# Chunk recurrence: corrections in two sets, a turned PE loop, new orders on DVE, ACT and GpSimd, a smaller filler

## The chip, the cores and the metric

The kernel runs on one core of a Trainium2 chip. A core has five engines with an instruction queue each: PE (TensorE, matmuls and the loading of their weights), DVE (VectorE), ACT (ScalarE), POOL (GpSimd) and SP (SyncE, which here issues transfers). They run on their own and wait for one another on semaphores. The metric is device time in microseconds (us), the median over runs.

## What is computed

Four images of 256 channels and 32 x 32 positions pass two residual layers; both see a group normalisation of their input. The first is the one that the change touches. Its tokens (4 x 1024) are projected to queries, keys and values of 8 heads with 32 columns, and a recurrence over 64 chunks of 16 tokens carries a small matrix `W1` (32 x 32) and a row `b1` for every head and image:

```python
def step(carry, inp):
    W1c, b1c = carry
    xq, xk, xv, et = inp
    Z1 = xk @ W1c + b1c
    grad = _ln_l2_bwd(Z1, xv - xk, g, bb)
    Attn1 = jnp.tril(xq @ xk.swapaxes(-1, -2))
    b1_bar = b1c - jnp.tril(et) @ grad
    Z1_bar = xq @ W1c - et * Attn1 @ grad + b1_bar
    last_eta = et[..., -1, :, None]
    W1n = W1c - (last_eta * xk).swapaxes(-1, -2) @ grad
    b1n = b1c - (last_eta * grad).sum(-2, keepdims=True)
    return ((W1n, b1n), xq + _ln(Z1_bar, g, bb, EPS_IN))
...
x = x + _L0_conv_ref(_gn(x), ...)   # the recurrence, then a layer norm and a projection
x = x + _L1_conv_ref(_gn(x), ...)   # a 5 x 5 self-correlation, a 1 x 1 convolution, relu
```

`grad` is the gradient of a layer norm's squared error: it needs the row sums of `Z1` and of its square, and two more sums of products.

## The kernel before

All 32 pairs of image and head are worked on together: a tile of a chunk has 128 partitions (4 groups of 2 heads x 16 tokens) and 4 x 32 = 128 columns (images x head columns). Ahead of the recurrence stand the group norm, the layer norm and the projections; behind it a layer norm, the output projection and the second layer. In the recurrence every engine runs one list of instructions, chunk after chunk, in an order written out by hand; semaphores in the dictionary `q` carry a count for each step. Only PE has a loop there: chunks 0 and 1, then a loop whose body holds four chunks (it runs 15 times, with a branch back after each), then chunks 62 and 63. The other engines' lists are written out for all 64 chunks.

In chunk c the steps run as follows (names as in the code, lines as in the profile).

- PE, function `body`: waits for the gradient `GL` of chunk c-1 (count `gl`), its mask products (`am`) and ACT's copy of the key products (`s1`). It then adds the correction by that gradient to `Z` of chunk c, which already stands in a PSUM bank (`grads`, L1167, 32 matmul passes); updates `W1` and `b1` (`update`, L1179 and L1187); adds the attention part to the queries' bank of chunk c-1 (`grads` again, L1167); issues `filler`, a matmul of the identity by 256 columns whose result nobody reads (L1194, two passes); computes `base`, that is `Z` of chunk c+1 by the state so far with the products of its keys (L1152) and the bias (L1158); and `qbase`, the queries of chunk c by the state (L1231). The branch back of the loop stands after `qbase`, ahead of the corrections.
- ACT: the square of `Z` (L1556); `out_store`, which copies a finished transposed chunk `ZT` into `TT` (L1548); a square for the output norm (L1538); a root (L1562) and a variance (L1565); copies of the new `W1` and `b1` from PSUM for PE (L1497, L1501); in chunks 40 to 47 a `gain` over 512 columns (L803); then keys and queries for later matmuls (L1508 two instructions, L1524 two, L1517) and `products`, the copy of the key products of chunk c+1 that is counted in `s1` (L1531); last a root for the output norm (L1544).
- DVE: sums of the square and of `Z` (L1300, L1301), `PZ`, `ZC`, `TS` (L1302 to L1308), a reciprocal (L1314), `y` (L1319), `yp`, `my`, `m` (L1322 to L1325), two 4-wide products `cc0` and `cc1` (L1328, L1332), `YC` (L1336), `WX` (L1338), and the gradient `GL` = `WX` + `YC` (L1341). Behind it, for older chunks: a sum for the output norm (`out_var`, L1284), `out_turn` (the transposition of `ZN` into `ZT`, L1294) and `out_rows` (L1279).
- POOL: `u`, `u2` (L1423, L1426) and `YL` (L1428); in chunk 56 a `pre` over 512 columns (L1449); `blocks`, the keys of chunk c+2 spread for PE's `base` (L1395); `masks`, the mask products of chunk c+1 (L1411); `out_norm`, which writes `ZN` of chunk c-3 (L1419) once the turn of chunk c-4 has read it; `queries`, a copy for chunk c+2 (L1403).
- SP issues transfers that wait for counts of `gl` and `khx`.

## Time and profile before

| what | us |
|---|---|
| median of 3 runs (583.01 to 584.29) | 583.49 |
| the profiled run | 581.06 |
| its span, first to last instruction | 579.2 |
| chunk 0's square to the last gradient | 282.71 |

The profile is one execution on the chip. Each row of its timeline has a start and a duration in us from the span's start, the engine, the line of the program, the operation, what it writes and reads, the count of instructions merged into the row and, in brackets, how long the engine had been idle and what ended that. PE is the matmuls and PEld the loading of weights; matmuls overlap one another, and their ends are modelled. "issue" as a releaser means that the profile shows nothing that was waited for. The granted clock is a share of 2.4 GHz.

### The profile page before, as it was taken

How to read it: one execution, taken by the hardware profiler on the slowest of the kernel's cores; microseconds unless marked ns; L12 is line 12 of the kernel's file. 1: busy time of each engine (PE TensorE's matmuls, PEld its weight loads, DVE VectorE, ACT ScalarE, POOL GpSimd, SP SyncE). 2: the span in 40 equal slices, each digit the busy share in tenths (PEclk: the TensorE clock that was granted, in tenths of full speed). 3: DMA queues.
4: the chain of work that ended last, by engine and by line, in shares of the span. 5: the costliest groups of instructions: out<-in, count | busy, mean ns of one | idle time of the engine just before them, and what ended most of it. 6: DMA issues, size and time to landing. Idle time of an engine off the chain costs nothing.

```text
span 579.2 us, 30352 instructions
## 1 busy us (share of the span) xinstructions
PE 483.9 (84%) x12556; PEld 313.8 (54%) x12556; DVE 432.1 (75%) x1526; ACT 346.2 (60%) x1166; POOL 327.8 (57%) x590
## 2 busy tenths in 40 slices
PE   0699889898558789888888888888887699998996
PEld 0344334443346577777777676666675244456563
DVE  4757788888746789888888888888885667676652
ACT  2344334322246788888888889988885487553321
POOL 1276888787734466666666655565763667330112
PEclk9999989899858999999999999999997899998998
DMA  8310111111101011111111000011010500000123
GB/s 338 123 24 14 37 37 36 38 36 36 39 9 32 22 37 28 33 32 33 33 28 37 1 1 1 19 36 37 19 37 4 171 1 2 1 2 1 74 75 145
DMA packets 15136, 24.74 MB, mean 43 GB/s; under 512 B 4228, under 2 KB 4968, under 8 KB 15080
## 3 DMA queue, kind: packets, MB, share of 16 engines
q1 hardware_dynamic: 15080, 24.10, 13.8%
q8 instruction: 23, 0.38, 0.3%
q14 instruction: 33, 0.27, 0.2%
HBM read 11.50 MB, written 4.19 MB: 27 GB/s over the span
## 4 chain that ended last, share of the span: by engine, by line
PE 25%; DVE 24%; ACT 12%; issue 8%; POOL 2%; POOLq 0%; ACTq 0%
PE PS L1167 6%; PE PS L924 4%; PE PS L1255 3%; PE PS L906 3%; ACT work L1556 3%; PE PS L361 2%; DVE work L1341 2%; DVE work L1336 2%; DVE work L1322 2%; DVE work L1300 2%; DVE work L1319 2%; DVE PS L1338 2%; DVE PS L1323 2%; DVE PS L1302 2%; DVE PS L1325 2%
## 5 line engine op out<-in xcount | busy, mean ns | idle before, releaser
L1167 PE MATMUL PS<-work 32*32 32x32 f32 x4064 | 59.6, 194 | 37.9 <-DVE work L1341 21.0
L1167 PEld LDWEIGHTS PS<-work 32*32 32x32 f32 x4064 | 53.8, 108 | 43.4 <-issue 43.1
L1411 POOL TENSOR_TENSOR work<-work,mask 128x256 f32<-128x256 f32 x64 | 46.8, 731 | 35.7 <-ACT work L1531 35.7
L512 PE MATMUL PS<-X,work 128*128 128x512 f32 x128 | 63.2, 641 | 0.3 <-ACT X L435 0.3
L1423 POOL TENSOR_TENSOR work<-work,lrh 128x4 f32<-128x4 f32 x64 | 12.9, 201 | 75.6 <-DVE work L1314 70.1
L1300 DVE TENSOR_REDUCE work<-work 128x4 f32<-128x128 f32 x64 | 18.3, 286 | 49.2 <-ACT work L1556 49.2
L663 POOL TENSOR_TENSOR work<-work 128x512 f32<-128x512 f32 x32 | 43.8, 1370 | 7.1 <-DVE work L582 7.1
L1152 PEld LDWEIGHTS PS<-work 64*32 64x32 f32 x2048 | 32.9, 110 | 24.9 <-issue 23.6
L1152 PE MATMUL PS<-work 64*32 64x64 f32 x2048 | 43.6, 225 | 2.9 <-issue 2.0
L1194 PE MATMUL PS<-cst 128*128 128x256 f32 x126 | 45.1, 440 | 0.0
L1179 PE MATMUL PS<-work 32*64 32x32 f32 x2016 | 43.0, 222 | 2.2 <-issue 2.2
L1508 ACT ACTIVATE work<-TK,small 128x128 f32<-128x128 f32 x128 | 44.3, 402 | 0.0
L1524 ACT ACTIVATE work<-QP,cst 128x128 f32<-128x128 f32 x128 | 43.9, 396 | 0.0
L1395 POOL TENSOR_TENSOR work<-KP,cst 128x256 f32<-128x256 f32 x64 | 39.2, 612 | 6.5 <-POOLq L454 6.5
L512 PEld LDWEIGHTS PS<-X,work 128*128 128x128 f32 x128 | 25.3, 206 | 29.5 <-issue 28.7
L881 POOL TENSOR_TENSOR TK<-TK 128x512 f32<-128x512 f32 x7 | 9.0, 1304 | 53.5 <-ACT TK L1077 53.5
L1179 PEld LDWEIGHTS PS<-work 32*64 32x64 f32 x2016 | 35.8, 135 | 3.9 <-issue 1.3
L581 DVE TENSOR_TENSOR work<-PS,work 128x512 f32<-128x512 f32 x32 | 21.8, 683 | 21.4 <-POOL KP L666 19.1
L1544 ACT ACTIVATE work<-work,small 128x4 f32<-128x4 f32 x64 | 19.0, 296 | 24.7 <-DVE work L1284 24.6
L377 ACT ACTIVATE work<-X 128x512 f32<-128x512 f32 (+1 forms) x16 | 9.7, 630 | 40.0 <-DVE X L368 40.0
L1255 PE MATMUL PS<-TK,wsm 128*128 128x512 f32 x64 | 31.4, 616 | 1.5 <-ACT X L1600 1.5
L1158 PE MATMUL PS<-work,cst 128*128 128x128 f32 x128 | 32.2, 334 | 0.0
(162 smaller groups left out, 1344.5 us busy)
## 6 DMA issues: line engine op xcount, KB each, us to landing
X<-in_x SPq DMA_DIRECT2D x4, 1024.0 KB, 8.2
TK<-KP SPq DMA_DIRECT2D x64, 64.0 KB, 1.9
X<-QP SPq DMA_DIRECT2D x64, 64.0 KB, 2.0
TK<-in_x SPq DMA_DIRECT2D x16, 256.0 KB, 3.0
out<-TK SPq DMA_DIRECT2D x16, 256.0 KB, 2.4
work<-in_rope SPq DMA_DIRECT2D x2, 512.0 KB, 9.1
cst<-in_consts SPq DMA_DIRECT2D x1, 289.0 KB, 5.0
work<-in_wk SPq DMA_DIRECT2D x1, 256.0 KB, 11.2
```

Source lines behind the costliest of these rows:

```text
L512: mm = nc.tensor.matmul(PS[:, 2 + m, :], lhs(j), xt(i, j), start=(j == 0), stop=(j == J - 1))
L663: nc.gpsimd.tensor_tensor(ksw[:, t, :], ksw[:, t, :], sinT[:, h], ALU.mult).then_inc(s_ksin, 1)
L1152: mm = nc.tensor.matmul(PS[HD * a:HD * a + HD, ZB[p], b * ZW:b * ZW + ZW], KT2[p][r:r + 64, k * B + b, :, :].rearrange("p e t -> p (e t)") ...
L1158: nc.tensor.matmul(PS[:, ZB[p], 0:B * ZW].rearrange("p (b n) -> p b n", b=B)[:, :, 0:HD], ident, Bs[1 - p if past(n, 1) else 0], start=Fal ...
L1167: mm = nc.tensor.matmul(PS[HD * a:HD * a + HD, bank, b * width:b * width + HD], AM[p][HD * a:HD * a + HD, b, part, :, :].rearrange("p e t ...
L1179: mm = nc.tensor.matmul(PS[2 * HD * a2:2 * HD * a2 + 2 * HD, WB + k, b * HD:b * HD + HD], KHX[p][HD * a:HD * a + HD, b, :, :].rearrange("p ...
L1194: nc.tensor.matmul(PS[:, QB[p], 256:512], ident, ccol("spread", 0, 256), start=True, stop=True, skip_group_check=True)
L1255: mm = nc.tensor.matmul(PS[:, 2 + m, :], wsm[:, j, m * P:(m + 1) * P], ot(i, j), start=(j == 0), stop=(j == J - 1))
L1395: nc.gpsimd.tensor_tensor(KT2[p], chunk(KP, c).unsqueeze(2).broadcast_to([P, J * B, E, CS]), ccol("emask_k").unsqueeze(1).unsqueeze(3).bro ...
L1411: nc.gpsimd.tensor_tensor(AM[p].rearrange("p b s e t -> p (b s) e t"), S1[p].unsqueeze(2).broadcast_to([P, 2 * B, E, CS]), mask2.rearrange ...
L1508: kx = nc.scalar.activation(KHX[p][:, :, e, :].rearrange("p b (f t) -> p b f t", f=E), head_rows(1, c), ACT.Copy, scale=upd_mask[:, e:e + 1])
L1524: a = nc.scalar.activation(QT2[p][:, :, e, :], chunk(QP, c), ACT.Copy, scale=ccol("emask_k", e, 1))
```

## The change

- The corrections are two sets of 32 passes: `YC` first, once `yc`, `am` and `s1` are there, then `WX` once `w` is there. `GL` is still computed, for `update` and the attention part, which now wait for `gl`. `WX` moves from PSUM to SBUF.
- PE's body is cut into `front` (corrections, update, attention, filler) and `back` (`base`, `qbase`), and the loop runs back, front: four backs and four fronts a pass, with the branch back after a front. Prologue and epilogue are written out around it.
- `filler` has 128 columns instead of 256, and the fourth front of each pass has none; nor has the one after the loop.
- DVE: `my` ahead of `yp`, `cc0` and `YC` ahead of `cc1`, `out_var` between `WX` and `GL`.
- `out_turn` writes `TT` itself; ACT's `out_store`, the tile `ZT` and the counts `zt` are gone, and `out_norm` waits for `ot`.
- POOL: after `YL` come `out_norm` and `queries`, then a wait for `gl` of this chunk, `masks`, `blocks`.
- ACT: the two `qt2` copies (L1524) stand behind `products`.

The diff, cut to its core:

```diff
@@ -776,8 +776,8 @@
             return PS[:, 7, at * B * HD:(at + 1) * B * HD].rearrange("p (b d) -> p b d", b=B)
 
 
-        PZ, WX, ZC = (home(at) for at in range(3))
-        at = 3 * B * HD
+        PZ, ZC = (home(at) for at in range(2))
+        at = 2 * B * HD
         cc0, sums = PS[:, 7, at:at + B], PS[:, 7, at + B:at + 3 * B]
 
...
@@ -1191,39 +1181,15 @@
 
                 def filler(p):
 
-                    nc.tensor.matmul(PS[:, QB[p], 256:512], ident, ccol("spread", 0, 256), start=True, stop=True,
+                    nc.tensor.matmul(PS[:, QB[p], 256:384], ident, ident, start=True, stop=True,
                                      skip_group_check=True)
 
...
-                run_chunks(pe, body)
+                def front(p, before, done, now, fill):
+
+                    o = 1 - p
+                    pe.wait_ge(q["init"], 1)
+                    pe.wait_ge(q["yc"], done)
+                    pe.wait_ge(q["am"], done)
+                    pe.wait_ge(q["s1"], now)
+                    grads(ZW, ZB[p], o, 1, YC)
+                    pe.wait_ge(q["init"], 1)
+                    pe.wait_ge(q["w"], done)
+                    grads(ZW, ZB[p], o, 1, WX).then_inc(q["corr"], 1)
+                    pe.wait_ge(q["init"], 1)
+                    pe.wait_ge(q["gl"], done)
+                    pe.wait_ge(q["khx"], done)
+                    pe.wait_ge(q["bcopy"], done)
+                    update(o)
+                    grads(HD, QB[o], o, 0, GL[o]).then_inc(q["attn"], 1)
+                    if fill:
+                        if before is not None:
+                            pe.wait_ge(q["zq"], before)
+                        filler(p)
+
+                def back(c, p, before, now, nxt):
+
+                    if not is_last(c):
+                        base(c + 1, 1 - p, nxt, now)
+                    else:
+                        pe_mean(pe, 0, True)
+                    query_base(now, p, before)
+
+                base(0, 0, 1, 1)
+                back(0, 0, None, 1, 2)
+                front(1, None, 1, 2, True)
+                back(1, 1, None, 2, 3)
+                front(0, 1, 2, 3, True)
+
+                with nc.Fori(0, NC // 4 - 1, engines=(mybir.EngineType.PE,), hint_back_edge=True) as four:
+                    for k in range(4):
+                        c, p = four * 4 + (2 + k), k % 2
+                        before, done, now, nxt = (value(pe, c + n) for n in (-1, 0, 1, 2))
+                        back(c, p, before, now, nxt)
+                        front(1 - p, done, now, nxt, k < 3)
+                back(NC - 2, 0, NC - 3, NC - 1, NC)
+                front(1, NC - 2, NC - 1, NC, False)
+                back(NC - 1, 1, NC - 2, NC, None)
...
@@ -1291,8 +1301,9 @@
                 def out_turn(c):
 
                     dve.wait_ge(q["zn"], c + 1)
-                    nc.vector.transpose(ZT.rearrange("p b d -> p (b d)"), ZN.rearrange("p b d -> p (b d)")
-                                        ).then_inc(q["zt"], 1)
+                    nc.vector.transpose(
+                        TT.rearrange("p e (b n) -> p b e n", b=B)[:, :, :, c * CS:(c + 1) * CS],
+                        ZN.rearrange("p b (e t) -> p b e t", e=E)).then_inc(q["ot"], 1)
 
                 def body(c, p):
                     zb = PS[:, ZB[p], 0:B * ZW].rearrange("p (b n) -> p b n", b=B)[:, :, 0:HD]
...
                     dve.wait_ge(q["y"], c + 1)
                     dve.wait_ge(q["zc"], c + 1)
+                    nc.vector.tensor_reduce(sums[:, 0:B], YY[:, 0, :, :], AX.X, ALU.add).then_inc(q["my"], 1)
                     nc.vector.tensor_tensor(YY[:, 1, :, :], YY[:, 0, :, :], ZC, ALU.mult).then_inc(q["yp"], 1)
-                    nc.vector.tensor_reduce(sums[:, 0:B], YY[:, 0, :, :], AX.X, ALU.add).then_inc(q["my"], 1)
-                    dve.wait_ge(q["yp"], c + 1)
-                    nc.vector.tensor_reduce(sums[:, B:2 * B], YY[:, 1, :, :], AX.X, ALU.add).then_inc(q["m"], 1)
                     dve.wait_ge(q["u"], c + 1)
                     dve.wait_ge(q["my"], c + 1)
                     nc.vector.scalar_tensor_tensor(cc0, sums[:, 0:B], -1.0 / HD, lead[:, 0, :],
                                                    ALU.mult, ALU.mult).then_inc(q["cy"], 1)
+                    dve.wait_ge(q["yp"], c + 1)
+                    nc.vector.tensor_reduce(sums[:, B:2 * B], YY[:, 1, :, :], AX.X, ALU.add).then_inc(q["m"], 1)
+                    dve.wait_ge(q["yl"], c + 1)
+                    dve.wait_ge(q["cy"], c + 1)
+                    nc.vector.tensor_tensor(YC, YL, bc(cc0), ALU.add).then_inc(q["yc"], 1)
                     dve.wait_ge(q["m"], c + 1)
                     dve.wait_ge(q["u2"], c + 1)
                     nc.vector.scalar_tensor_tensor(cc1, sums[:, B:2 * B], -1.0 / HD, lead[:, 1, :],
                                                    ALU.mult, ALU.mult).then_inc(q["c"], 1)
-                    dve.wait_ge(q["yl"], c + 1)
-                    dve.wait_ge(q["cy"], c + 1)
-                    nc.vector.tensor_tensor(YC, YL, bc(cc0), ALU.add).then_inc(q["yc"], 1)
                     dve.wait_ge(q["c"], c + 1)
                     nc.vector.tensor_tensor(WX, ZC, bc(cc1), ALU.mult).then_inc(q["w"], 1)
-                    dve.wait_ge(q["w"], c + 1)
                     dve.wait_ge(q["yc"], c + 1)
-                    nc.vector.tensor_tensor(GL[p], WX, YC, ALU.add).then_inc(q["gl"], 1)
-
                     if past(c, 2):
                         out_var(c - 2)
+                    dve.wait_ge(q["w"], c + 1)
+                    nc.vector.tensor_tensor(GL[p], WX, YC, ALU.add).then_inc(q["gl"], 1)
+
                     if past(c, 4):
                         out_turn(c - 4)
                     if past(c, 1):
...
@@ -1415,7 +1422,7 @@
 
                 def out_norm(c, p):
                     if past(c, 1):
-                        pool.wait_ge(q["zt"], c + 0)
+                        pool.wait_ge(q["ot"], c + 0)
                     nc.gpsimd.tensor_tensor(ZN, ZQ[c % 3], bc(sdq[1 - p]), ALU.mult).then_inc(q["zn"], 1)
...
@@ -1428,14 +1435,16 @@
                     nc.gpsimd.tensor_tensor(YL, YY[:, 0, :, :], bc(lead[:, 0, :]), ALU.mult).then_inc(q["yl"], 1)
                     if c == PRE_AT:
                         pre(0)
-                    if not near_end(c):
-                        blocks(c + 2, p)
-                    if not is_last(c):
-                        masks(c + 1, 1 - p)
                     if past(c, 3):
                         out_norm(c - 3, 1 - p)
                     if not near_end(c):
                         queries(c + 2, p)
+
+                    pool.wait_ge(q["gl"], c + 1)
+                    if not is_last(c):
+                        masks(c + 1, 1 - p)
+                    if not near_end(c):
+                        blocks(c + 2, p)
 
                 for c in range(2):
...
-
                 def body(c, p):
                     zb = PS[:, ZB[p], 0:B * ZW].rearrange("p (b n) -> p b n", b=B)[:, :, 0:HD]
                     if past(c, 1):
                         act.wait_ge(q["corr"], c + 0)
                     nc.scalar.activation(SQ, zb, ACT.Square).then_inc(q["sq"], 1)
-                    if past(c, 5):
-                        out_store(c - 5)
                     if past(c, 2):
...
@@ -1573,12 +1574,11 @@
                         act.wait_ge(q["ot"], NC // PER)
                         gain(act, i, j).then_inc(q2["in"], 1)
                     khx(c, p)
-                    if not is_last(c):
-                        qt2(c + 1, 1 - p)
                     if not isinstance(c, int) or c + 3 < NC:
                         next_k(c + 2, p)
                     if not is_last(c):
                         products(c + 1, 1 - p)
+                        qt2(c + 1, 1 - p)
                     if past(c, 2):
                         out_sd(c - 2, p)
 
```

## Rows read from the trace of the kernel before

**Rows 1.** Busy time by stretch: us, five engines' busy time (instructions), clock, DMA share, GB/s.
```profile
167.69:199.27 31.58, 23.13 (x942) 18.02 (x938) 20.64 (x101) 20.67 (x81) 15.09 (x40) 0.86 0.12 29
199.27:433.48 234.21, 203.83 (x9469) 162.56 (x9470) 201.42 (x990) 198.35 (x834) 147.37 (x387) 1.00 0.10 25
433.48:450.40 16.92, 13.31 (x422) 9.82 (x419) 10.36 (x52) 9.05 (x38) 5.82 (x17) 0.80 0.02 6
```

**Rows 2.** Timeline of one steady chunk (start, us, engine, line, operation, operands, count).
```profile
253.48 0.28 ACT L1556 ACTIVATE work<-PS 128x128 f32<-128x128 f32 x1
...
254.18 0.47 PE L1167 MATMUL PS<-work 32*32 32x32 f32 x32
...
254.50 0.42 ACT L1497 ACTIVATE work<-PS 128x128 f32<-128x128 f32 x2
...
254.58 0.70 PE L1194 MATMUL PS<-cst 128*128 128x256 f32 x2
254.58 0.29 DVE L1308 TENSOR_TENSOR work<-TK,work 128x128 f32<-128x128 f32 x1
254.78 0.20 DVE L1314 RECIPROCAL work<-work 128x8 f32<-128x8 f32 x1
...
255.06 0.20 POOL L1423 TENSOR_TENSOR work<-work,lrh 128x4 f32<-128x4 f32 x1 [1.03 <-DVE work L1314]
...
255.21 0.65 PE L1152 MATMUL PS<-work 64*32 64x64 f32 x32
...
255.85 0.61 POOL L1395 TENSOR_TENSOR work<-KP,cst 128x256 f32<-128x256 f32 x1
...
256.30 0.29 DVE L1338 TENSOR_TENSOR PS<-PS,work 128x128 f32<-128x128 f32 x1
256.34 0.36 ACT L1531 ACTIVATE work<-PS,small 128x128 f32<-128x128 f32 x1
256.63 0.29 DVE L1341 TENSOR_TENSOR work<-PS,work 128x128 f32<-128x128 f32 x1
256.77 0.73 POOL L1411 TENSOR_TENSOR work<-work,mask 128x256 f32<-128x256 f32 x1 [0.31 <-ACT work L1531]
...
257.02 0.45 PE L1167 MATMUL PS<-work 32*32 32x32 f32 x32 [0.36 <-DVE work L1341]
257.03 0.30 DVE L1294 STREAM_TRANSPOSE work<-work 128x128 f32<-128x128 f32 x1
...
257.40 0.67 PE L1179 MATMUL PS<-work 32*64 32x32 f32 x32
257.46 0.40 POOL L1419 TENSOR_TENSOR work<-work 128x128 f32<-128x128 f32 x1
257.54 0.28 ACT L1556 ACTIVATE work<-PS 128x128 f32<-128x128 f32 x1
...
257.80 0.29 POOL L1403 COPY work<-QP 128x128 f32<-128x128 f32 x1
```

**Rows 3.** Timeline in a chunk with `gain`: products, and the corrections that they release.
```profile
349.22 0.36 ACT L1531 ACTIVATE work<-PS,small 128x128 f32<-128x128 f32 x1
...
349.72 0.45 PE L1167 MATMUL PS<-work 32*32 32x32 f32 x32 [0.88 <-ACT work L1531]
```

**Rows 4.** Timeline: the first corrections behind the loop's branch back.
```profile
265.62 0.45 PE L1167 MATMUL PS<-work 32*32 32x32 f32 x32 [0.83 <-POOL work L1411]
```

**Rows 5.** Busy time by stretch: chunks 2 to 5, the loop's first pass.
```profile
178.68:199.27 20.59, 15.59 (x697) 12.13 (x698) 14.21 (x70) 13.91 (x58) 10.22 (x28) 1.00 0.12 29
```

**Rows 6.** Timeline: corrections of chunk 62, just behind the loop.
```profile
437.13 0.32 PE L1167 MATMUL PS<-work 32*32 32x32 f32 x15 [0.47 <-DVE work L1341]
440.55 0.44 PE L1167 MATMUL PS<-work 32*32 32x32 f32 x17 [3.11 <-issue]
```

**Rows 7.** Timeline in chunk 57, where POOL is late by its `pre`.
```profile
416.33 0.62 POOL L1395 TENSOR_TENSOR work<-KP,cst 128x256 f32<-128x256 f32 x1
...
416.67 0.42 DVE L1308 TENSOR_TENSOR work<-TK,work 128x128 f32<-128x128 f32 x1
```

69 lines of the change are left out of this document (12 added, 57 removed).

## Prediction

> **What bounds the kernel now.** I read first the busy time by stretches [rows 1]. The span of 579.2 us falls into a front part (167.69 us), the recurrence over 64 chunks (282.71 us, cut here at the squares of chunk 0, 6 and 61 and at the last gradient) and a back part (128.80 us). Only the recurrence is edited. In its middle stretch 55 chunks take 234.21 us, 4.26 each, with no engine busy all the time: a loop of waits, not an engine, sets the pace.
>
> Second, the timeline of one steady chunk [rows 2]. Let S be the start of the ACT square L1556, 253.48; the next is at 257.54, so a chunk is 4.06. The loop that ends last runs square, sums and elementwise work on DVE, WX (L1338, S+2.82), GL (L1341, S+3.15 to 3.44), the correction matmuls L1167 (S+3.54), next square. But three others are close behind, and the whole question is which comes next:
> - ACT and PE: state copy L1497 ends at S+1.44, base L1152 at S+1.73 (just when the filler L1194 lets it go), products L1531 1.13 after it, S+2.86 to 3.22. They let the corrections go 0.14 later [rows 3], at S+3.36, so 0.18 of slack against S+3.54.
> - GpSimd: the key blocks L1395 at S+2.37, masks L1411 at S+3.29, query normalisation L1419 0.69 later. The blocks are done more than two us before the base that reads them. That is much slack.
> - PE itself: in every fourth chunk the loop jump stands between the query base and the corrections; L1167 is then idle 0.83 [rows 4] in place of 0.36 [rows 2], so that chunk costs 0.47 more: four chunks 4 x 4.06 + 0.47 = 16.71.
>
> Third, the two ends. The first pass over PE code is slow: 1395 matmuls and weight loads in 20.59 us [rows 5], 14.8 ns each, four chunks at 5.15. Where PE leaves the loop, it stops 3.11 us inside a correction, waiting for nothing that is recorded [rows 6], and the clock of that stretch is 0.80 on the mean [rows 1].
>
> **The change part by part.**
>
> *Two-set corrections.* GL (WX + YC) leaves the path: PE takes YC first, then WX. On DVE the same instructions stand between the sums and WX; `my` now needs a finished `y` and the two 4-wide products stand apart, so WX starts some 0.06 later, at S+2.88, ends S+3.17 and could reach PE at S+3.27 (GL to L1167 took 0.10 [rows 2]). Alone this would shorten the chunk by 0.27. But PE has 32 matmuls more, 0.38 (L1167 to L1179 [rows 2]), and the first set waits for the products too.
>
> *The ACT and PE loop then.* The 128-column filler takes half of 0.63, so it ends at S+1.41 and no longer holds the base; the state copy does: 1.44 + 0.14 = S+1.58. The products follow 1.13 after it, as before, with the bias between them: S+2.71. ACT is free by then, as the two query copies now stand behind the products. Products 0.36, to PE 0.14: the YC set starts at S+3.21, the WX set at S+3.59, and its square follows 0.52 later (257.02 to 257.54): 4.11. WX had been ready 0.3 earlier. So what GL gives, the second set takes: 4.11 against 4.06.
>
> *GpSimd's new order.* Normalisation and query copy now come before masks and blocks, and the masks get a wait for GL. Queued behind that wait are masks and blocks; the base of the next chunk waits for the blocks. Yet the added wait is not the late one: `out_norm(c-3)` waits for `out_turn(c-4)`, which DVE runs after GL(c). Before, blocks and masks filled that time; now they queue behind it. WX S+2.88, two DVE slots (0.40 for two, L1341 to L1294) to GL at 3.28, turn 3.48 to 3.78, to GpSimd 0.08 (L1314's end to L1423): normalisation S+3.86, copy +0.35, masks +0.29, blocks +0.69 at S+5.19, done S+5.80, PE 0.14 later: S+5.94. If the next chunk starts at S+4.11, that is its +1.83, and its base was wanted at +1.58. From base to the following square is 4.11 - 1.58 = 2.53, so two chunks cost 8.47, not 8.22.
>
> *TS under the blocks.* The blocks now run at +1.08 to +1.69 of the next chunk, just when DVE's TS (L1308) starts at +1.10. The one place of the trace where blocks and TS overlap shows TS at 0.42 us [rows 7], against 0.29 in the steady chunk [rows 2]: +0.13, which everything up to the turn inherits: 8.60 for two chunks. The Trainium skill, "SBUF — State Buffer", section "SBUF: two separate sides", calls the port pair of VectorE and GpSimd an exclusive lock, also for a VectorE operation with two SBUF inputs, as TS is; by that rule TS would end only after the blocks, up to 0.45 later, and the fours below would cost about 0.3 more. The one overlap agrees in kind.
>
> *Turned loop.* The jump now stands between the attention matmuls and the base. Attention L1167 ends at S+1.17 (254.18 + 0.47); plus 0.83 is S+2.00 against 1.58: +0.42 in that chunk, which has no filler. It stays on the path: the pair with it is 2 x 4.11 + 0.42 = 8.64. Four chunks: 8.64 + 8.60 = 17.24, or 17.11 without the TS stretch, against 16.71. For some 47 ordinary chunks (64 less 6 at the head, 8 with `gain`, 3 at the tail), 11.75 fours: +4.7 to +6.2. I take +5.5, nearer to the end with the stretch, since a row shows it.
>
> *Chunks with gain* (8): there the products are last (idle 0.88 before L1167 [rows 3], so 4.58). From the state copy to the products ACT works 1.84 without a break on eight instructions [rows 2]; two of them move behind, an estimate of 0.5. With the second set (+0.38) that leaves -0.15 a chunk: -1.2 in all (0 to -2).
>
> *First pass.* 64 PE instructions more a chunk at 14.8 ns: 0.95 for each of four chunks in the loop, and 0.8 for chunk 1 and the loop's new entry: +4.6. Bounds: +1, if this code is not what PE waits for, to +6.
>
> *Tail.* The exit now comes after front 62, so one front less is left for new code. The 3.11 stall may stand before the base of chunk 62 instead (gain 0) or vanish with the low clock behind it: 16.92 against three chunks of 4.2 and 0.3, so -4. I take -3, as PE ran on for 15 matmuls past the exit before it stopped. The Trainium skill, "Runtime: NRT & Kernel Launch", "Instruction fetch mechanics", has instructions come in blocks of 256; by that the rest of chunk 62 would be at hand already, which speaks for the lower end.
>
> *At nothing.* The ACT store (0.30) goes; ACT waits for the first sum after it anyway. The turn writes TT in 16-element runs: no row shows that on DVE; ACT wrote the same runs in 0.30 and TS reads them in 0.29, so 0, with 0.1 as upper bound (+2.4 in all). WX in SBUF: 0, other operands of this shape differ by 0.01. SP's transfers wait for GL counts that come within 0.2 of before; nothing waits for them here.
>
> *Sum.* +4.6 + 5.5 - 1.2 - 3.0 = +5.9. The profiled run took 581.06 (span 579.2), 2.4 below the median 583.49 of the runs; so 587.0 for that run and 589.4 for the median.
>
> **The rivals.**
> 1. *The jump hides and GpSimd is in time (faster).* If PE's sequencer turns the loop while the attention matmuls run, and the blocks end before S'+1.44, only the 4.11 loop is left: fours of 16.44, -3.2 in 47 chunks, gains -1.5, tail -4, head +4: about -5, 578.5. It decides at whether the blocks end before the state copy. Against: the addition above misses that by 0.25, and the jump showed 0.83 of idle.
> 2. *It does what it says.* If the products are no limit and WX is last: -0.27 for some 58 chunks, -0.44 for 13 jumps, +4.6 at the head, -3 at the tail: -19.8, 563.7. Against: [rows 3] show the products letting PE go.
> 3. *The larger loop no longer stays at hand.* Four chunks hold 4 x 64 instructions more than now. If each pass must fetch its code again, each costs 1632 x 14.8 ns = 24.2 against 17.2, 14 times: +98; if only its first piece, 3.11 x 14 = +44: 630 to 690. For: first pass and exit show what fetching costs. Against: after its first pass, the present loop shows clock 1.00 and no such stop over 55 chunks. The skill's section on fetching gives PE room for 2048 instructions; about 1670 fit, if not by much in whole blocks.
> 4. *The clock falls to 1.2 GHz,* with a quarter and more of the filler gone. About 2.0 us of the 4.11 are PE's and would at most double; a tenth of the 64 chunks would be +12: 601. Against: the clock is 1.00 over the middle stretch, with jumps (idle 0.83) and gain chunks (0.88) in it, and 32 matmuls are added.
>
> **How the numbers follow.** Forecast 0.70, with 584 to 594 as its own range (head +1, no TS stretch; tail 0, turn 0.1 dearer); rival 1 0.12; rival 2 0.04; rival 3 0.08; rival 4 0.06. Some 0.2 % (1.2 us) is what a measurement can tell from no change. Faster: rivals 1 and 2 and a little of the forecast, 0.18; same: the forecast's lower end, 0.10; slower 0.72. The range 577.0 to 598 leaves out rivals 2 and 3, a quarter of rival 1 and most of rival 4.
>
> **What would show it.** Right: squares some 4.1 and 4.3 to 4.6 apart by turns, base released by GpSimd's blocks or the jump, the YC set by the products, GpSimd's normalisation by the turn, TS longer than 0.29. Wrong: squares 3.8 apart with the WX set released by L1338's successor; jump chunks no longer than others; stops of 3 us within the middle stretch; a clock below 1.00 there.

## The result, and the profile after

The changed kernel takes 597.85 us (median of four runs, 596.37 to 600.41) against 583.89 of before in the same comparison: ratio 1.0238, 95 % interval 1.0191 to 1.0285. The forecast was 589.4, slower by 5.9; it is slower by 14.0. The direction and the steady chunk were right, the size was not. The profiled execution of the changed kernel took 600.41 with a span of 598.6, against 581.06 and 579.2. Runs of one kernel of this family differ by up to some 3 % with the mean granted clock (one below took 583.21 at 0.941 and 601.41 at 0.906), so differences are read from stretches whose clock stands beside them.

First the busy time by stretch, cut at the ACT squares (L1559 now) of chunks 0, 6, 12, 57 and 60 and at the last gradient; then the stretch that the trace shows at the lower clock behind the first pass, the middle, and the one behind chunk 57. Columns as in [rows 1].

```profile
166.93:205.78 38.85, 29.00 (x1130) 24.31 (x1126) 20.38 (x101) 20.59 (x80) 15.05 (x40) 0.68 0.10 24
205.78:236.46 30.68, 28.59 (x1228) 24.45 (x1229) 21.59 (x108) 20.62 (x85) 14.37 (x39) 0.72 0.09 22
236.46:431.68 195.22, 170.84 (x9162) 145.52 (x9162) 172.58 (x811) 158.18 (x638) 121.34 (x317) 1.00 0.09 24
431.68:449.73 18.05, 16.05 (x615) 13.62 (x618) 11.01 (x55) 10.35 (x43) 10.19 (x26) 0.62 0.09 28
449.73:467.58 17.85, 15.02 (x685) 11.77 (x686) 14.27 (x71) 11.97 (x50) 8.51 (x23) 0.94 0.02 6
...
199.19:223.08 23.89, 23.05 (x754) 19.56 (x754) 14.30 (x72) 13.30 (x54) 9.46 (x26) 0.50 0.08 20
223.08:434.71 211.63, 184.78 (x9931) 157.58 (x9927) 185.66 (x875) 171.23 (x693) 131.74 (x342) 1.00 0.09 24
434.71:448.36 13.65, 12.92 (x443) 10.86 (x433) 8.77 (x45) 6.99 (x28) 6.35 (x18) 0.50 0.05 19
```

Beside the same cuts of before (its squares stand at 167.69, 199.27, 224.14, 415.57 and 429.41, its last gradient at 450.40):

| stretch | before | after | difference | forecast |
|---|---|---|---|---|
| ahead of chunk 0 | 167.69 | 166.93 | -0.8 | 0 |
| chunks 0 to 5 | 31.58 | 38.85 | +7.3 | +4.6 |
| chunks 6 to 11 | 24.87 | 30.68 | +5.8 | +0.7 |
| chunks 12 to 56 | 191.43 | 195.22 | +3.8 | +3.1 |
| chunks 57 to 59 | 13.84 | 18.05 | +4.2 | +0.4 |
| chunk 60 to the last gradient | 20.99 | 17.85 | -3.1 | -2.9 |
| behind | 128.8 | 131.0 | +2.2 | 0 |

(The forecast column spreads the +5.5 of 47 ordinary chunks evenly, and adds the -1.2 of the gain chunks to chunks 12 to 56.) Chunks 12 to 56 and the last ones up to the gradient agree within 0.7. The two that miss by most are those with a mean clock of 0.72 and 0.62: at 1.2 GHz TensorE is busy 23.05 of 23.89 us and sets the pace by itself, 6.1 us a chunk. The first six chunks (mean clock 0.68) miss by 2.7 and the part behind the recurrence by 2.2.

The timeline of two steady chunks, from square to square to square (the form of [rows 2]; the chunk of 4.16, then one of 4.48), with the base of the chunk ahead of them, which stands behind the jump:

```profile
264.43 0.65 PE L1142 MATMUL PS<-work 64*32 64x64 f32 x32 [0.90 <-POOL work L1402]
...
266.83 0.28 ACT L1559 ACTIVATE work<-PS 128x128 f32<-128x128 f32 x1 [0.17 <-PE PS L1157]
...
267.81 0.61 POOL L1402 TENSOR_TENSOR work<-KP,cst 128x256 f32<-128x256 f32 x1
...
267.93 0.64 DVE L1319 TENSOR_TENSOR work<-TK,work 128x128 f32<-128x128 f32 x1
...
268.52 0.65 PE L1142 MATMUL PS<-work 64*32 64x64 f32 x32
...
269.63 0.37 ACT L1540 ACTIVATE work<-PS,small 128x128 f32<-128x128 f32 x1 [0.42 <-PE PS L1148]
...
270.14 0.78 PE L1157 MATMUL PS<-work 32*32 32x32 f32 x64 [0.16 <-ACT work L1540]
...
270.63 0.30 DVE L1304 STREAM_TRANSPOSE TK<-work 128x128 f32<-128x128 f32 x1
...
270.99 0.28 ACT L1559 ACTIVATE work<-PS 128x128 f32<-128x128 f32 x1
271.02 0.40 POOL L1426 TENSOR_TENSOR work<-work 128x128 f32<-128x128 f32 x1 [1.42 <-DVE TK L1304]
...
272.09 0.40 DVE L1319 TENSOR_TENSOR work<-TK,work 128x128 f32<-128x128 f32 x1
...
272.30 0.67 POOL L1402 TENSOR_TENSOR work<-KP,cst 128x256 f32<-128x256 f32 x1
...
273.06 0.65 PE L1142 MATMUL PS<-work 64*32 64x64 f32 x32 [0.48 <-POOL work L1402]
...
274.17 0.37 ACT L1540 ACTIVATE work<-PS,small 128x128 f32<-128x128 f32 x1 [0.79 <-PE PS L1148]
...
274.68 0.74 PE L1157 MATMUL PS<-work 32*32 32x32 f32 x64 [0.16 <-ACT work L1540]
...
275.47 0.28 ACT L1559 ACTIVATE work<-PS 128x128 f32<-128x128 f32 x1 [0.16 <-PE PS L1157]
```

Read it against the forecast. The products L1540 let all 64 corrections go 0.14 after their end (TensorE was idle 0.16 by then); WX and GL are no longer last. GpSimd's normalisation L1426 waits 1.42 for DVE's turn L1304, so the key blocks L1402 come at +0.98 and +1.31 of the chunk, the base waits for them (S+2.07 in the second), and DVE's TS L1319 beside them takes 0.64 and 0.40 in place of 0.29 [rows 2]. The pair is 4.16 + 4.48 = 8.64; four chunks, one pass of the loop and called a four below, take 17.28. The forecast had 17.24, by the same steps.

### The profile page after: what moved, and what is told of

It reads as the page before. It is cut to its first block, busy times and chain, and to the rows that moved or that the text cites. A ratio compares the mean times of both kernels' runs of the same rounds, so it can differ in the third digit from the quotient of the medians.

```text
span 598.6 us, 34394 instructions
## 1 busy us (share of the span) xinstructions
PE 503.0 (84%) x14540; PEld 342.3 (57%) x14540; DVE 438.8 (73%) x1526; ACT 338.5 (57%) x1102; POOL 328.9 (55%) x590
## 3 DMA queue, kind: packets, MB, share of 16 engines
HBM read 11.50 MB, written 4.19 MB: 26 GB/s over the span
## 4 chain that ended last, share of the span: by engine, by line
PE 33%; issue 13%; POOL 13%; DVE 7%; ACT 6%; POOLq 0%; ACTq 0%
PE PS L1157 6%; PE PS L1142 4%; PE PS L924 4%; PE PS L1265 3%; PE PS L361 3%; PE PS L1148 3%; POOL work L1418 3%; POOL work L1402 3%; PE PS L906 3%; ACT work L1540 2%; POOL work L1426 2%; PE PS L1169 2%; POOL work L1435 2%; PE PS L946 1%; ACT work L1559 1%
## 5 line engine op out<-in xcount | busy, mean ns | idle before, releaser
L1157 PE MATMUL PS<-work 32*32 32x32 f32 x6080 | 82.5, 198 | 16.4 <-ACT work L1540 9.4
L1157 PEld LDWEIGHTS PS<-work 32*32 32x32 f32 x6080 | 76.7, 111 | 22.3 <-issue 21.2
L1426 POOL TENSOR_TENSOR work<-work 128x128 f32<-128x128 f32 x64 | 25.6, 400 | 90.4 <-DVE TK L1304 89.0
L1142 PE MATMUL PS<-work 64*32 64x64 f32 x2048 | 46.2, 233 | 22.4 <-POOL work L1402 18.0
L1142 PEld LDWEIGHTS PS<-work 64*32 64x32 f32 x2048 | 36.7, 116 | 31.9 <-issue 30.0
L1540 ACT ACTIVATE work<-PS,small 128x128 f32<-128x128 f32 x64 | 23.5, 367 | 48.2 <-PE PS L1148 47.8
L1169 PE MATMUL PS<-work 32*64 32x32 f32 x2016 | 45.3, 228 | 2.6 <-issue 2.4
L1402 POOL TENSOR_TENSOR work<-KP,cst 128x256 f32<-128x256 f32 x64 | 40.8, 637 | 5.8 <-POOLq L454 5.8
L1169 PEld LDWEIGHTS PS<-work 32*64 32x64 f32 x2016 | 39.0, 142 | 6.1 <-issue 2.5
L1148 PE MATMUL PS<-work,cst 128*128 128x128 f32 x128 | 34.6, 356 | 0.0
L1197 PE MATMUL PS<-work 64*32 64x32 f32 x2048 | 31.0, 202 | 0.7 <-issue 0.7
```

The lines of the kernel that those rows point to most:

```text
L1142: mm = nc.tensor.matmul(PS[HD * a:HD * a + HD, ZB[p], b * ZW:b * ZW + ZW], KT2[p][r:r + 64, k * B + b, :, :].rearrange("p e t -> p (e t)") ...
L1148: nc.tensor.matmul(PS[:, ZB[p], 0:B * ZW].rearrange("p (b n) -> p b n", b=B)[:, :, 0:HD], ident, Bs[1 - p if past(n, 1) else 0], start=Fal ...
L1157: mm = nc.tensor.matmul(PS[HD * a:HD * a + HD, bank, b * width:b * width + HD], AM[p][HD * a:HD * a + HD, b, part, :, :].rearrange("p e t ...
L1169: mm = nc.tensor.matmul(PS[2 * HD * a2:2 * HD * a2 + 2 * HD, WB + k, b * HD:b * HD + HD], KHX[p][HD * a:HD * a + HD, b, :, :].rearrange("p ...
L1402: nc.gpsimd.tensor_tensor(KT2[p], chunk(KP, c).unsqueeze(2).broadcast_to([P, J * B, E, CS]), ccol("emask_k").unsqueeze(1).unsqueeze(3).bro ...
L1426: nc.gpsimd.tensor_tensor(ZN, ZQ[c % 3], bc(sdq[1 - p]), ALU.mult).then_inc(q["zn"], 1)
```

## The experiments

**The filler's size.** The first question was whether the clock at half belongs to the smaller filler.

```
-PS[:, QB[p], 256:384], ident, ident, ...
+PS[:, QB[p], 256:512], ident, ccol("spread", 0, 256), ...
```

> The changed kernel with one size put back: the filler has 256 columns again, still in the same three of four chunks. Theory A (the smaller filler lets TensorE's clock fall in the first pass over the loop and behind the GpSimd stop of chunk 57): the granted clock is back at 1.00 by about chunk 5, the squares of chunk 0 and chunk 12 are 60 us apart in place of 69.5, the three chunks behind chunk 57's square take 14 in place of 18, and the steady fours stay at 17.3 (a filler twice as long ends at S+1.8, which only the chunks without late key blocks notice, +0.1): about 587 to 589 in all. Theory B (the stops of the longer first pass over new code hold the clock down, whatever the filler): the clock stays at 0.50 over chunks 5 to 8, 598 to 601.

Measured: 595.73 (594.93 to 596.24), ratio 1.0181. Chunks 6 to 11 took 26.1 (first row below) and chunks 57 to 59 13.89, at clock 1.00 both, as theory A has it; but chunks 0 to 5 still took 37.6, and in the middle stretch the clock fell twice, at chunks 22 and 42. So A holds for the stretch behind the first pass, and not for the first pass itself, and its total of 587 to 589 was missed. No filler at all:

```
-front(1 - p, done, now, nxt, k < 3)
+front(1 - p, done, now, nxt, False)
...
-front(1, None, 1, 2, True)
+front(1, None, 1, 2, False)
...
-front(0, 1, 2, 3, True)
+front(0, 1, 2, 3, False)
```

> The changed kernel without any filler matmul (the filler only writes a part of a bank that nothing reads). Theory A3 (the filler is what brings TensorE's clock back after a stop; with 256 columns chunks 6 to 11 took 26.1, with 128 columns 30.7): it stays at 0.50 for longer behind the first pass and behind chunk 57 than with 128 columns, and the middle stretch is no longer at 1.00 throughout either; chunks 6 to 11 take 33 or more, the total is over 605. Rival (the filler has nothing to do with it; the falls come by chance behind each stop): 592 to 600, chunks 6 to 11 at 30 to 31; the steady chunks gain nothing, as the base waits for the key blocks or the jump.

Measured: 602.09 (601.60 and 602.58). The clock fell in the middle stretch too, in chunks 36 and 52, mean 0.89 over 206.76 us. Chunks 6 to 11 took 28.7, not 33, and the total stayed below 605: these numbers of the theory missed. And the filler in all four chunks:

```
-front(1 - p, done, now, nxt, k < 3)
+front(1 - p, done, now, nxt, True)
...
-front(1, NC - 2, NC - 1, NC, False)
+front(1, NC - 2, NC - 1, NC, True)
...
-PS[:, QB[p], 256:384], ident, ident, ...
+PS[:, QB[p], 256:512], ident, ccol("spread", 0, 256), ...
```

> The changed kernel with the 256-column filler in all four chunks and in the last fronts too. Against the kernel with 256 columns in three of four (595.7, chunk with the jump 4.37 to 4.57). Theory of the forecast (the jump begins only when TensorE has done what stands before it, so the filler's 0.70 adds to it): the base behind the jump starts at about S+2.8 in place of S+2.1, one chunk in four grows by some 0.5, 599 to 602 if the clock holds as well. Rival (the sequencer turns the loop while the long matmul runs): base still at S+2.1, 592 to 596.

Measured: 593.66 (590.97 to 595.77). The rival won: the jump runs beside the long matmul. Busy time of chunks 6 to 11 with 256 columns, then of the middle stretch without filler, with 256 columns in three of four and in all four:

```profile
204.83:230.91 26.08, 23.13 (x1225) 19.12 (x1228) 22.25 (x108) 20.19 (x84) 14.36 (x40) 1.00 0.10 26
...
231.50:438.26 206.76, 172.38 (x9095) 149.09 (x9096) 170.60 (x811) 158.49 (x639) 122.42 (x320) 0.89 0.08 23
...
230.91:429.56 198.65, 180.15 (x9163) 147.79 (x9167) 169.43 (x810) 156.76 (x639) 121.48 (x317) 0.97 0.09 24
...
230.06:426.09 196.03, 183.38 (x9184) 148.09 (x9185) 170.42 (x810) 156.75 (x638) 121.33 (x317) 1.00 0.09 24
```

TensorE's timeline without filler, in chunk 36 (where the clock falls: the same 32 matmuls take 0.94, then 1.07; no jump stands there, the base waits for GpSimd's key blocks), then at the jump, in chunk 18, with 256 columns in three of four, and in all four:

```profile
337.18 0.94 PE L1142 MATMUL PS<-work 64*32 64x64 f32 x32 [0.89 <-POOL work L1402]
...
342.57 1.07 PE L1142 MATMUL PS<-work 64*32 64x64 f32 x32
...
258.93 0.65 PE L1142 MATMUL PS<-work 64*32 64x64 f32 x32 [0.93 <-POOL work L1402]
...
257.29 0.70 PE L1184 MATMUL PS<-cst 128*128 128x256 f32 x2
258.33 0.65 PE L1142 MATMUL PS<-work 64*32 64x64 f32 x32 [0.34 <-POOL work L1402]
```

From attention matmuls to base it is 1.39 without the filler (257.54 to 258.93) and 1.43 with it (256.90 to 258.33): 0.70 of matmul cost 0.04. (The key blocks end 0.22 to 0.26 ahead of these two bases. In the single-set kernels below they are done 3 us earlier, and the same distance is 1.40 without the filler, 1.43 and 1.37 with it.) TensorE then stands idle 0.34 at the jump, not 0.93, and in this kernel the clock stayed at 1.00 from chunk 6 to chunk 61. Even so it takes 11.0 more than the kernel before (593.66 against 582.65): its profiled execution has +4.2 over before's in chunks 0 to 5, +1.8 in chunks 6 to 11, +4.6 in chunks 12 to 56, -2.1 from chunk 60 on and +3.4 behind the recurrence.

The same small filler in the kernel before:

```
-PS[:, QB[p], 256:512], ident, ccol("spread", 0, 256), ...
+PS[:, QB[p], 256:384], ident, ident, ...
...
-body(four * 4 + (2 + k), k % 2)
+body(four * 4 + (2 + k), k % 2, k > 0)
```

> The kernel before with the filler of the change alone: 128 columns, in the same three of four chunks. Theory A (filler): the clock falls to 0.50 in the first pass or behind chunk 57 here too, and the time rises by 4 to 13, to 588 to 597; the steady chunks stay at 4.06, since there the gradients are last and not the base. Theory B (code stops of the longer first pass): the clock stays as in the kernel before, 584 within 1.

Measured: 615.03 (600.02 to 619.34), ratio 1.0538, more than either expectation. The middle stretch of the profiled execution (600.02) reads:

```profile
224.45:434.80 210.35, 185.90 (x7727) 156.14 (x7728) 164.44 (x810) 165.66 (x684) 121.06 (x317) 0.81 0.08 23
```

A mean of 0.81 over 210.35 us is 80 us at 1.2 GHz, nearly all in chunks 42 to 56, where chunks of 4.06 to 4.59 became 4.65 to 6.38. Its first pass is that of before (31.41 against 31.58). So the small filler lets the clock fall, and does nothing to the first pass.

**The changed kernel once more,** without an edit, to see what of the clock is fixed by the program.

> The changed kernel itself, a second profiled execution. If the falls of the clock are fixed by the program, it falls again at the same places (chunks 3, 5 to 8, 57 to 59), 597 to 600. If they depend on how a stop happens to fall in time, the steady chunks are again 4.16 and 4.47 by turns, but the length at 0.50 behind the first pass and behind chunk 57 differs from the first execution, and so does the time, by up to 6.

Measured: 593.60 and 603.75. The steady chunks are again 4.16 and 4.47 by turns; chunks 6 to 11 again took 31, at a mean clock of 0.71; but behind chunk 57 nothing fell this time (12.5 us for three chunks), and two falls in chunks 18 and 54 took its place (mean clock 0.93 over chunks 12 to 56, where the first execution had 1.00). So where it falls is left to the execution.

**GpSimd's order.** Back to the order of before, first without and then with the wait for GL ahead of the masks.

```
+blocks(c + 2, p)
+masks(c + 1, 1 - p)
 out_norm(c - 3, 1 - p)
 queries(c + 2, p)
-pool.wait_ge(q["gl"], c + 1)
-masks(c + 1, 1 - p)
-blocks(c + 2, p)
```

> The changed kernel with GpSimd's order of before alone: key blocks, masks, output normalisation, query copy, without the wait for GL. Theory of the forecast (the order sets the steady pace by the late blocks and by the lengthened TS): TS L1319 back at 0.29, base at S+1.6 in three of four chunks and at S+2.1 behind the jump, fours of 16.5 in place of 17.26, some 12 fours, so 588 to 590 if the clock of the first pass stays as it is. Rival (the two sets or the turned loop set the pace by themselves): fours of 17.1 to 17.3, 596 to 598.

Measured: 588.34 (584.06 to 598.46), ratio 1.0069: the time as expected, the fours not quite, 16.93 (3.99, 4.19, 3.99, 4.76) for 16.5. What was missing shows in the timeline: GL, whose operands all lie in SBUF now, runs beside the masks.

```profile
257.18 0.77 DVE L1354 TENSOR_TENSOR work<-work 128x128 f32<-128x128 f32 x1
...
257.07 0.73 POOL L1418 TENSOR_TENSOR work<-work,mask 128x256 f32<-128x256 f32 x1
```

```
+blocks(c + 2, p)
 pool.wait_ge(q["gl"], c + 1)
 masks(c + 1, 1 - p)
-blocks(c + 2, p)
+out_norm(c - 3, 1 - p)
+queries(c + 2, p)
```

> The changed kernel with GpSimd's order of before, but with the wait for GL kept ahead of the masks: key blocks, wait, masks, output normalisation, query copy. With the order of before alone, GL L1354 took 0.77 in place of 0.28 in every chunk in which the masks ran beside it, and the next base came 0.2 later. Theory (the stretch is caused by the masks beside it, since GL's operands all lie in SBUF now): GL back at 0.28, chunks of 3.99 in three of four and about 4.5 behind the jump, fours of 16.5 in place of 16.93, some 583 in all. Rival (the stretch has another cause, or the masks now come too late for the corrections that need them): fours of 16.9 or more, 588 or more.

Measured: chunks of 3.99 to 4.03 and 4.66 to 4.70 behind the jump, a four of 16.68, and GL back at its length, as the row of that line says (duration min/median/max in ns):

```profile
L1354 DVE TENSOR_TENSOR work<-work x64: 281/283/544, 171.2 to 468.3; 128x128 f32<-128x128 f32 x64
```

The theory holds for the chunk, and the total missed: 591.13 (583.21 to 601.41), ratio 1.0100. In the profiled execution (601.41) the clock fell in chunks 6 and 57 and, with 0.87 to 0.88 of idle at the jump, in chunks 10, 22 and 34. The port rule of the Trainium skill, "SBUF — State Buffer", section "SBUF: two separate sides", fits here: GL started 0.11 behind the masks and ended just behind them. It fits the changed kernel's TS of 267.93 too, which began 0.12 behind the key blocks and ended 0.15 behind them. It fits less well with the TS of 272.09, which began 0.21 ahead of the key blocks and still took 0.40 for 0.29.

**The loop turned back.**

```
-back(c, p, before, now, nxt)
-front(1 - p, done, now, nxt, k < 3)
+front(p, before, done, now, k < 3)
+back(c, p, before, now, nxt)
```

> The changed kernel with the loop unturned: the branch back stands again between the query base and the corrections, all else as changed. Theory of the forecast (the jump costs 0.4 to 0.5 in its chunk wherever it stands; in the turned loop the late key blocks hide part of it): fours of 17.3 to 17.8, 598 to 604. Rival (turning is what lost time: the jump ahead of the base is dearer than ahead of the corrections): fours below 17.0, 592 to 595.

Measured: 608.81 (604.76 to 612.97), ratio 1.0431. Fours at clock 1.00 took 17.4 (4.90, 4.00, 4.37, 4.16) to 17.9, about as the theory has it, the total beyond it: the chunk without filler leaves 0.90 of idle ahead of its base and the jump 0.77 behind it, and the clock fell behind three of these pairs. The turn of the loop is no loss here.

**The first pass.** TensorE idles 7.6 us ahead of the recurrence; nine long matmuls there keep its clock up to chunk 0.

```
+for n in range(9):
+    nc.tensor.matmul(PS[:, 6, :], ident, ccol("spread", 0, 512), ...
```

> The changed kernel with nine matmuls of 512 columns into an unread bank on TensorE just ahead of the recurrence, where it idles 7.6 us between L566 and L1123 and its clock falls. Theory A2 (the first pass is slow because it begins at 1.2 GHz, with little work between its stops): the granted clock is 1.00 from the square of chunk 0 on, the squares of chunk 0 and 12 are 57 to 61 us apart in place of 69.5, and the total is 586 to 590. Theory B (the code stops of the first pass pull the clock down again, or the stops themselves are what costs): the clock falls to 0.50 in the first pass all the same, and the total is 594 to 600.

Measured: 596.94 (593.83 to 602.44). Chunk 1 fell from 7.43 to 6.10, but the clock was at 0.50 again from 168.52 on, still in chunk 0, in which TensorE waits 3.00 for DVE, and chunks 0 to 11 took 65.4. Theory B. With GpSimd's order and the wait for GL as well:

```
+for n in range(9):
+    nc.tensor.matmul(PS[:, 6, :], ident, ccol("spread", 0, 512), ...
...
+blocks(c + 2, p)
 pool.wait_ge(q["gl"], c + 1)
 masks(c + 1, 1 - p)
-blocks(c + 2, p)
+out_norm(c - 3, 1 - p)
+queries(c + 2, p)
```

> Both together: GpSimd's order of before with the wait for GL, and the nine matmuls ahead of the recurrence. If both theories hold, fours of 16.5 and the squares of chunk 0 and 12 some 58 us apart: 575 to 579, faster than either kernel. If only the order counts, 583; if neither, 590 or more.

Measured: 594.47 (589.23 to 602.02), no gain: three falls behind jumps (chunks 18, 26, 46), chunks 0 to 11 at 67.1.

**Two sets alone,** on the kernel before.

```
-pe.wait_ge(q["gl"], done)
...
-grads(ZW, ZB[p], o, 1).then_inc(q["corr"], 1)
+pe.wait_ge(q["yc"], done)
...
+grads(ZW, ZB[p], o, 1, YC)
+pe.wait_ge(q["w"], done)
+grads(ZW, ZB[p], o, 1, WX).then_inc(q["corr"], 1)
+pe.wait_ge(q["gl"], done)
```

> The kernel before with the two-set corrections alone (YC's set, then WX's, with WX in SBUF); its orders, its loop and its 256-column filler stay. Theory of the forecast (the products release the corrections 0.14 later, and the second set takes 0.38 more): chunks of 4.1 to 4.3, since the masks run beside GL here and stretch it, which delays the update; fours of 16.9 to 17.3, the first pass 3 to 9 longer for its 64 more PE instructions a chunk: 590 to 597. Rival (taking GL off the path pays): chunks of 3.8 to 3.9, 576 to 581.

Measured: 598.81 (598.26 to 600.66), ratio 1.0293, somewhat above the 597 of the theory. The chunk is 4.19, 4.83 with the jump, 4.86 with gain; at clock 1.00 the middle stretch took 200.2 against 191.4. The first six chunks took 39.7. By itself the second set costs as much as the whole change. The masks began only at GL's end here, so the stretch of GL that I expected did not occur.

**The change without its two sets.** Single set, GpSimd and VectorE orders of before, 256 columns in three of four; turned loop, query copies behind the products, and the turn without ACT store stay.

```
-grads(ZW, ZB[p], o, 1, YC)
-pe.wait_ge(q["w"], done)
-grads(ZW, ZB[p], o, 1, WX).then_inc(q["corr"], 1)
+grads(ZW, ZB[p], o, 1, GL[o]).then_inc(q["corr"], 1)
```

> The change without its two-set corrections, its GpSimd order and its small filler: one set of corrections from GL (WX in PSUM, the VectorE order of before), the 256-column filler in three of four, the turned loop, the query copies behind the products, the turn straight into TT with no ACT store. From the rows: the steady chunk stays at 4.06, since GL is last; the jump now stands where the filler stood, so the base behind it starts at S+2.0 in place of S+1.73, the products let the corrections go at S+3.63 in place of S+3.54: 0.1 in place of 0.47 in one chunk of four, -4.3 in all; the chunks with gain lose 0.80 of ACT work ahead of the products, 4.58 to 4.2, -3; tail -3; the first pass as before. If the falls of the clock come from the code that two sets add and from the small filler, 572 to 576. If the turned loop by itself lets the clock fall, 582 or more.

Measured: 584.80 (581.24 to 590.53), ratio 1.0033 [1.0008, 1.0058]. The chunks are as expected: 4.06, and 4.18 to 4.24 behind the jump (before 4.5), gain chunks 4.06 to 4.4 (before 4.58). The time is not: the clock fell behind the jumps of chunks 26 and 38, 2.3 us each, and again at the end. So the filler went into the chunk with the jump too:

```
-front(1 - p, done, now, nxt, k < 3)
+front(1 - p, done, now, nxt, True)
...
-front(1, NC - 2, NC - 1, NC, False)
+front(1, NC - 2, NC - 1, NC, True)
```

> The single-set turned kernel with the 256-column filler in all four chunks and in the last front. With the filler in three of four its steady chunks were 4.06 and 4.24, but the clock fell at two jumps (chunks 26 and 38, 2.5 us each) and for 17 us from the last chunks into the back part. Theory (TensorE's clock falls where it stands idle at a jump or a stop with no long matmul beside it; the jump itself runs while the long matmul runs, so this filler costs nothing): no fall of the clock in the middle stretch, chunks behind the jump 4.2 to 4.3, the back part at 129 to 131 in place of 134.4: 574 to 578, faster than both kernels. Rival (the falls have nothing to do with the filler behind the jump, or the filler adds to the jump): 583 to 588.

Measured: 576.45 (575.06 to 577.66), ratio 0.986 [0.9819, 0.9901]. The theory holds in the middle; the back part came down to 132.5 only.

The nine matmuls ahead of the recurrence in this kernel too:

```
+for n in range(9):
+    nc.tensor.matmul(PS[:, 6, :], ident, ccol("spread", 0, 512), ...
```

> The same with the nine matmuls of 512 columns ahead of the recurrence. In the two-set kernel these took chunk 1 from 7.43 to 6.10, while the chunks of the loop's first pass stayed as slow. Theory (the first pass is limited by its code; the clock at its start counts for chunk 1 alone): 0 to 1.5 us faster than without them. Rival (with the code of before and a warm start the clock holds through the first pass): 3 to 5 us faster.

Measured: 573.96 (572.79 to 575.10), ratio 0.9817 [0.9777, 0.9857], the best of all. The time is between the two expectations, and its place is neither's: chunk 0 began 3.4 us earlier (164.52 against 167.94), the first pass was no shorter. Last, the two sets put into this kernel, and with them what the change has for them: `WX` in SBUF, VectorE's new order, and GpSimd's wait for GL ahead of the masks.

```
-grads(ZW, ZB[p], o, 1, GL[o]).then_inc(q["corr"], 1)
+grads(ZW, ZB[p], o, 1, YC)
+pe.wait_ge(q["w"], done)
+grads(ZW, ZB[p], o, 1, WX).then_inc(q["corr"], 1)
...
+pool.wait_ge(q["gl"], c + 1)
```

> The last kernel with the two-set corrections put in again (and GpSimd's wait for GL ahead of the masks, which keeps GL short): turned loop, 256 columns in all four chunks, nine matmuls ahead. If the clock holds here too, this is the price of the two sets alone. Theory of the forecast (the products let the corrections go and the second set adds 0.38; the first pass has 64 PE instructions more a chunk): chunks of 4.1 to 4.2 and 4.6 behind the jump, fours of 17.0 in place of 16.42, +7 in the middle stretch, +4 to +7 in the first pass: 584 to 588 against 574. Rival (with everything else mended the two sets pay): fours of 16.4 or less, 570 to 576.

Measured: 591.20 (588.98 to 593.50), ratio 1.0159; 17.2 over its twin, and beyond the 584 to 588 of the theory. The middle stretch of the single-set kernels (filler in three of four, with its two falls; in all four; the same with the nine matmuls), then of this one:

```profile
223.95:414.07 190.12, 165.94 (x7727) 134.13 (x7728) 164.51 (x810) 155.48 (x639) 119.34 (x315) 0.96 0.09 25
...
225.28:411.26 185.98, 167.46 (x7749) 133.29 (x7749) 164.57 (x810) 155.23 (x639) 119.36 (x315) 1.00 0.09 26
...
222.74:408.14 185.40, 167.47 (x7748) 133.30 (x7750) 164.57 (x810) 155.24 (x638) 119.39 (x315) 1.00 0.10 26
...
229.50:422.56 193.06, 182.24 (x9185) 147.68 (x9188) 160.47 (x810) 156.22 (x638) 119.78 (x316) 1.00 0.09 25
```

With the clock at 1.00, the two sets and what came with them cost 7.7 in 45 chunks (17.1 a four against 16.4), and 5.6 more in the first twelve (34.56 + 29.24 against 33.41 + 24.81), where the clock was not held. The kernel with the two sets alone says the same of the steady chunk, with VectorE's order of before: 200.2 against 191.4. So they do not pay with the clock held either.

## Why the prediction was right and wrong

**The steady chunk: right, by its own steps.** Products last, base released by key blocks or jump, normalisation held by the turn, TS stretched: all in the rows above; 17.28 a four for 17.24, chunks 12 to 56 +3.8 for +3.1. Two sizes inside cancel. The 64 corrections take 0.74 and their square comes 0.05 later, so the loop of the products alone is 4.00 (chunks 3.99 to 4.03 of the kernel with GpSimd's order and the wait for GL), where I had put 0.38 + 0.52 = 0.90 and 4.11. And the jump costs more than the 0.42 I gave it over that loop: 4.66 - 4.00 = 0.66.

**The gain chunks: right** (-1.57 for -1.2, though the sum there, -0.5 + 0.38, gives -0.12 a chunk and not -0.15), and so was **the tail** (-3.1 for -3.0): a stop of 1.57 in place of 3.11 [rows 6].

**The first pass: its price was about right, what followed it was left out.** For chunks 1 to 5 I had +4.6. The profiled executions of the twelve runs with two sets show +3.4 to +8.2 over the 26.5 of before, eight of them between 3.4 and 4.7; the changed kernel had +7.5, one of the two highest. Without two sets it is -0.2 to +1.8, in four runs. That each instruction costs 14.8 ns there was not tested, and what the stops wait for is not recorded. TensorE's timeline there, with its stops and an update at 1.2 GHz (1.08 for the 0.67 of [rows 2]), and at chunk 57 and in the tail:

```profile
187.12 0.42 PE L1169 MATMUL PS<-work 32*64 32x32 f32 x3 [2.43 <-issue]
...
195.33 0.65 PE L1142 MATMUL PS<-work 64*32 64x64 f32 x32 [1.11 <-issue]
...
199.31 0.31 PE L1157 MATMUL PS<-work 32*32 32x32 f32 x4 [1.65 <-issue]
...
205.65 1.08 PE L1169 MATMUL PS<-work 32*64 32x32 f32 x32
...
434.48 0.92 PE L1142 MATMUL PS<-work 64*32 64x64 f32 x32 [1.10 <-POOL work L1402]
...
463.40 0.58 PE L1157 MATMUL PS<-work 32*32 32x32 f32 x37 [1.57 <-issue]
```

**The step that failed is the clock: rival 4, for which the sum has no term.** I gave it 0.06 and argued against it from the middle stretch, where the clock is 1.00. It fell elsewhere: behind the stops of the first pass (199.19 to 223.08, chunks 5 to 8) and behind the base's wait of 1.10 for GpSimd in chunk 57. A chunk is then 5.75 to 6.31 in place of 4.16 or 4.48, some 1.8 more on the mean, near the 2.0 of rival 4. Chunks 6 to 11 and 57 to 59 carry +10.0 of the profiled difference where the forecast had +1.1; with the excess of 2.7 in chunks 0 to 5 that is 11.6 of the 13.5 by which the profiled execution passed the forecast (19.4 for 5.9); most of the rest is the back part's 2.2. (The median execution has 5.4 less of all this: 14.0 for 19.4.)

The rows of before held one warning, the 0.80 of [rows 1]: there the clock fell at 439.49, within the stop of 3.11 [rows 6]. The 0.86 at the head was none: the clock was low from 159.60, ahead of chunk 0, up to 176.67, and at 1.00 over the loop's first pass with its stops of 0.9 to 1.2 [rows 5]. Busy time and clock of before from there to chunk 6, then of the first 30 us behind the last gradient: before, the changed kernel, and the kernel without two sets with 256 columns in three of four:

```profile
159.60:176.67 17.07, 10.36 (x244) 8.30 (x244) 8.90 (x34) 8.70 (x31) 5.98 (x15) 0.50 0.07 16
176.67:199.27 22.60, 17.08 (x771) 13.28 (x766) 14.21 (x70) 14.28 (x59) 11.16 (x29) 1.00 0.11 28
...
450.40:480.40 30.00, 25.17 (x201) 10.94 (x201) 19.31 (x40) 20.63 (x41) 20.51 (x20) 0.94 0.27 82
...
467.58:497.58 30.00, 25.41 (x190) 10.35 (x188) 16.62 (x35) 17.56 (x34) 18.93 (x18) 0.87 0.29 82
...
445.73:475.73 30.00, 25.43 (x170) 10.48 (x170) 14.94 (x33) 15.28 (x29) 16.45 (x16) 0.74 0.28 84
```

What I carried over was a clock kept up with 256 columns of filler in every chunk. The change leaves 384 columns of 1024 in a pass, so five eighths are gone, which "a quarter and more" understates.

What the runs show of the cause: of the runs with two sets, the eight with 128 columns or none had a mean clock of 0.66 to 0.88 over chunks 6 to 11, and five of them 0.62 to 0.89 over chunks 57 to 59; the four with 256 columns had 1.00, 1.00, 1.00 and 0.88, and 1.00 in all four. The two sets' longer first pass seems to belong to it, as the kernel before with the small filler had 1.00 over chunks 6 to 11. In the middle stretch 14 falls were recorded, in seven runs with the turned loop and no filler ahead of the jump; every one began within 0.3 us of the start of a base that had stood idle 0.86 to 0.93. Twelve of these bases stand behind the jump; the two of the kernel without filler (chunks 36 and 52) wait for GpSimd's key blocks, with no jump there: what all 14 have in common is the idle time, not the jump. In the four kernels with 256 columns in all four chunks of the turned loop none was recorded. It is no law: most jumps of that idle time let the clock stand, and the kernel before, with 0.83 at its jump and 256 columns in each chunk, had none in its middle stretch. Why one jump and not the next, the runs don't tell.

The back part goes with the clock too: it took 128.3 to 129.3 in the four runs with a mean clock of 0.94 over the first 30 us behind the last gradient, and 130.6 to 134.4 in the thirteen with 0.74 to 0.88. The kernel with 256 columns in all four chunks bounds what the clock of the recurrence is worth: with it held from chunk 6 to 61 the time is 593.66 for 597.85, still 11.0 over before where the forecast had 5.9. Of what is left over the forecast, 3.4 stand in the back part of its profiled execution, at 0.85 over those 30 us.

**Rival 1** had the right mechanism and the wrong place for it: the jump does hide here, but behind a long matmul that stands ahead of it, and the change took just that one away. **Rival 2** fell with the kernel that differs in the two sets alone (chunks of 4.19 for 3.8). **Rival 3** did not occur: from 223 to 434 TensorE never stood idle for more than 0.94 us, which agrees with the room of 2048 instructions that the Trainium skill, "Runtime: NRT & Kernel Launch", "Instruction fetch mechanics", gives TensorE.

## What to carry to other kernels

Price a change of filler, or of TensorE's idle time, by the stretches of the trace that have stops, not by the steady stretch alone: a single idle of 0.9 us ahead of the base cost from 0.9 us (chunks 34 and 35 with GpSimd's order and the wait for GL) to more than 5 (chunks 36 to 40 without filler) here where the clock fell, and mostly nothing. A long matmul right ahead of the loop's jump was cheap here (0.04 us for 0.70 of matmul), so the chunk with the jump was the best place for the dummy. Splitting an accumulation to take one elementwise step off the path did not pay here, where something else, the products, came within that step's length of it.

## What the hardware showed that was not expected

At 1.2 GHz TensorE was busy 23.05 of 23.89 us with small matmuls, and the clock stayed at 0.50 all that time. An elementwise GL with all operands in SBUF took 0.77 us beside a GpSimd operation of 0.73 and 0.28 without it, and TS beside the key blocks 0.64 and 0.40 for 0.29. With nine long matmuls in TensorE's idle time ahead of the recurrence, chunk 0 began at 164.52 to 166.62 in four kernels; in the thirteen runs without them it began at 166.75 to 168.25.
